# A graph convolution whose end rows are turned and multiplied in strips of 128 columns

## The chip, the cores and the metric

The kernel runs on one core of a Trainium2 chip. The metric is the device time of one execution in microseconds (us). The engines are called TensorE (PE in the rows; PEld is its weight load), VectorE (DVE), ScalarE (ACT), GpSimd (POOL) and SyncE (SP, its DMA queue SPq). TensorE's clock is granted at one of two levels, shown as 0.5 (1.2 GHz) or 1.0 (2.4 GHz).

## What is computed

Four graph layers run one after the other on 12500 nodes with 64 features and 200000 edges, sorted by their target node: an attention layer, a gated layer, a polynomial layer and a block of three convolutions. The change touches the last:

```python
def conv(h, W, b):
    m = jnp.concatenate([h[dst], h[src], edge_attr], axis=1) @ W + b
    return jax.ops.segment_sum(m, dst, num_segments=n_nodes)
h = jax.nn.relu(conv(x, W1, b1))
h = jax.nn.relu(conv(h, W2, b2))
return conv(h, W3, b3)
```

The sum over the edges of a node can be drawn in front of the product. With deg the number of edges into a node, its output row is deg * (h @ W[0:64]) + (sum of h[src]) @ W[64:128] + (sum of the attributes) @ W[128:144] + deg * b. The kernel computes it in this way; the sums of the attributes are the same for all three convolutions.

## The kernel before, in words

Nodes lie in 98 tiles of 128 (`T` = 98), edges in 128 rows of `J` = 1564 columns, in 68 chunks of 23 columns (`NC`, `C`). `conv_layer` is called three times, with k = 0, 1, 2, and has a chunk part and an end part. All loops of it are unrolled; each engine has its own instruction stream, and semaphores order them.

*Chunk part.* GpSimd fetches h[src] for 23 columns, one indirect DMA of 128 rows a column (`gather_columns`, line 864), into one of two buffers. ScalarE (`take`, lines 2089 to 2097) spreads the flags that mark where a node's edges begin, brings in the 16 edge attributes where k is 0 (line 2096) and the gathered rows (2097). VectorE runs a segmented sum along the edges (2235: three scans of up to 32 features in the first convolution, two in the others). ScalarE puts the running sums back in row order (`give`, 2102) and SyncE stores them to a table in DRAM (2059), 80 columns wide in the first convolution and 64 in the others. In the first 33 chunks the node term is computed beside that, three tiles a chunk: ScalarE scales H by deg (`scale`, 2107; where k is over 0 it also copies 17 columns that hold the attribute sums and deg, 2109), TensorE turns the tile (2159), ScalarE copies it (2116), TensorE multiplies by `g.Wz` (2168), ScalarE copies the product into `z` (2121).

*End part.* A carry across the 128 edge rows is turned, scanned and turned back (2173, 2240, 2175), and one fixed row is corrected in the table (2023, 2247, 2025). Then GpSimd fetches for every tile the row at which each node's edges end, 98 indirect DMAs into `cat` (2032). Tiles are worked in units: eleven of 8 tiles, two of 4 and one of 2. For each unit TensorE turns the rows in PSUM (`turn_rows`), ScalarE copies them to SBUF (2147), TensorE multiplies (`multiply_rows`), VectorE adds `z` (2256) and, where k is 0, keeps the attribute sums (2261), ScalarE applies the ReLU (2140) and SyncE stores the unit (2067). TensorE's order is t0, then t(q+1) and m(q) for each unit q; the buffers form a ring of 2 where k is 0 and of 3 otherwise. ScalarE's order is copy(q), then ReLU(q-1).

The shapes differ. Where k is 0, each tile is 81 columns wide (64 sums, 16 attribute sums, deg), is turned by itself (2192) and multiplied by `g.Wt` with 64 output columns (2204). The column for deg is written into `cat` by VectorE once all chunks are stored (2244), and TensorE waits for that (`s_degs`). Where k is over 0, two tiles of 64 columns are turned at once (2188) and multiplied by a block diagonal of the weights in `g.Wkv` with 128 output columns (2200).

The weights of the convolutions are loaded in the first phase, near its end: twelve small DMAs on SyncE's queue (lines 433 to 440, issued by `load`, line 384), between the stores of a node table (422) that ScalarE's copies wait for (540).

## Time and profile before

| | us |
|---|---|
| median of 3 runs | 13276.4 |
| lowest and highest | 13261.65, 13276.62 |
| the profiled execution | 13250.52 |
| its span, first to last instruction | 13248.7 |
| busy: GpSimd | 9102.4 (69%) |
| busy: VectorE | 4039.7 (30%) |
| busy: ScalarE | 3484.7 (26%) |
| busy: TensorE | 1392.0 (11%) |

The page of the profile has the busy time of each engine, the costliest groups of instructions and the DMA queues. A busy share is a mean over phases with different limits. Which wait sets the end of a phase is read from the timeline, which lists instructions in order of time with the idle time before them and what ended it; "issue" there means that the profile shows nothing the engine waited for. Runs of like instructions are merged, with their count. A float32 product is recorded as two MATMUL instructions, and each has a LDWEIGHTS of its own.

### The profile page before, as it was taken

To read this page: it belongs to the slowest core of one execution; us is meant where nothing else is said; L and a number is where in the kernel's file an instruction comes from. 1 tells how busy PE (TensorE), PEld (TensorE's weight loads), DVE (VectorE), ACT (ScalarE), POOL (GpSimd) and SP (SyncE) were. 2 spreads that over 40 slices of the span, in tenths; PEclk is the share of its full clock that TensorE was granted. 3 is DMA by queue.
4 is the path that set the end of the run, shared out by engine and by line. 5 is a ranking of instruction groups with operands and counts; after the bars stand their busy time and mean duration, and the time that the engine had idled before them with its cause. 6 is when DMAs were issued, how large, how long until landed. Compare 5 with 4: busy or idle time off the path is not lost. (4 is left out here: it accounts for less than half of the span.)

```text
span 13248.7 us, 37564 instructions
## 1 busy us (share of the span) xinstructions
PE 1392.0 (11%) x6735; PEld 1006.9 (8%) x6735; DVE 4039.7 (30%) x5465; ACT 3484.7 (26%) x4624; POOL 9102.4 (69%) x8728
## 2 busy tenths in 40 slices
PE   5200000030000000395000000200000000000000
PEld 3100000010000000273000000100000000000000
DVE  2255555544544544695111111011111101111110
ACT  2322322312222222275332222122211212221121
POOL 4677777757777776402777777577777767777776
PEclk8655555555555555697555555555555555555555
DMA  7333333313333333001222222111111111111111
GB/s 283 132 99 95 95 100 96 95 31 89 94 99 95 94 94 87 14 1 31 62 58 61 58 58 58 42 50 46 49 46 46 48 39 50 46 49 46 46 48 42
DMA packets 404824, 919.06 MB, mean 69 GB/s; under 512 B 171046, under 2 KB 195277, under 8 KB 389496
## 3 DMA queue, kind: packets, MB, share of 16 engines
q0 software_dynamic: 278944, 386.91, 13.3%
q1 hardware_dynamic: 121832, 529.42, 10.9%
q14 instruction: 176, 1.44, 0.0%
q10 hardware_dynamic: 3824, 0.50, 0.0%
q8 instruction: 48, 0.79, 0.0%
HBM read 456.45 MB, written 459.77 MB: 69 GB/s over the span
## 5 line engine op out<-in xcount | busy, mean ns | idle before, releaser
L864 POOL DMA_INDIRECT arena<-tab,src x6256 | 6544.2, 1046 | 2893.7 <-issue 2103.0
L2235 DVE TENSOR_TENSOR_SCAN arena<-cv_keep,arena 128x768 f32<-128x768 f32 (+1 forms) x476 | 752.0, 1627 | 5754.5 <-issue 4533.5
L864 POOL DMA_INDIRECT arena<-tab,spread x1564 | 1651.7, 1056 | 510.2 <-issue 510.2
L2097 ACT COPY arena<-arena 128x1472 f32<-128x1472 f32 x204 | 545.3, 2673 | 3002.8 <-DMA arena<-tab,src 3002.8
L2102 ACT COPY arena<-arena 128x1472 f32<-128x1472 f32 (+1 forms) x204 | 588.4, 2884 | 552.4 <-DVE arena L2235 463.2
L1089 PE MATMUL e_t<-ident,arena 128*68 128x128 f32 (+1 forms) x2 | 0.8, 394 | 4426.1 <-PEq L1424 2216.7
L2159 PE MATMUL cv_t<-ident,arena 128*81 128x128 f32 (+1 forms) x294 | 138.0, 469 | 2912.8 <-ACT arena L2109 1671.9
L2096 ACT COPY arena<-arena 128x368 f32<-128x368 f32 x68 | 55.3, 813 | 1351.3 <-issue 1322.7
L2173 PE MATMUL cv_t<-ident,arena 128*64 128x128 f32 (+1 forms) x3 | 1.3, 425 | 3391.4 <-ACT arena L2102 3391.4
L951 ACT ACTIVATE ae_prob<-arena 128x92 f32<-128x92 f32 x68 | 17.1, 251 | 1228.4 <-issue 942.8
L1874 DVE TENSOR_SCALAR arena<-arena 128x448 bf16<-128x448 f16 x1252 | 325.2, 329 | 43.2 <-issue 21.1
L1493 DVE TENSOR_TENSOR arena<-arena,ge_small 128x23 f32<-128x23 f32 x68 | 13.3, 195 | 1065.3 <-DMA arena<-tab,src 1065.3
L1089 PEld LDWEIGHTS e_t<-ident,arena 128*68 128x68 f32 (+1 forms) x2 | 0.3, 131 | 4426.4 <-issue 4426.4
L1757 PE MATMUL po_u<-arena,Hn 128*128 128x448 bf16 x1564 | 301.4, 355 | 289.7 <-DVE Hn L1864 289.7
L1025 DVE TENSOR_TENSOR arena<-arena,ae_prob 128x1472 f32<-128x1472 f32 x68 | 260.1, 3825 | 219.6 <-issue 215.5
L1456 ACT ACTIVATE ge_decay<-arena 128x768 f32<-128x768 f32 x68 | 56.4, 830 | 1015.0 <-issue 902.1
L992 DVE TENSOR_TENSOR_SCAN ae_work<-ae_keep,arena 128x768 f32<-128x768 f32 x136 | 240.1, 1765 | 221.8 <-remote 146.6
L1757 PE MATMUL po_u<-arena 128*128 128x448 bf16 x1564 | 298.8, 352 | 0.2 <-DVE arena L1874 0.2
L943 ACT ACTIVATE ae_work<-arena 128x768 f32<-128x768 f32 x136 | 208.4, 1533 | 300.8 <-issue 261.0
L2159 PEld LDWEIGHTS cv_t<-ident,arena 128*81 128x81 f32 (+1 forms) x294 | 53.9, 183 | 2949.7 <-ACT arena L2109 1683.0
L1034 DVE TENSOR_TENSOR_SCAN arena<-ae_work,arena 128x768 f32<-128x768 f32 x136 | 238.8, 1756 | 115.2 <-issue 101.7
L1497 DVE TENSOR_TENSOR arena<-arena,ge_small 128x1472 f32<-128x1472 f32 x68 | 258.7, 3804 | 0.2 <-issue 0.2
(369 smaller groups left out, 7017.6 us busy)
## 6 DMA issues: line engine op xcount, KB each, us to landing
rows<-arena SPq DMA_DIRECT2D x68, 1506.5 KB
arena<-tab,src POOLq DMA_INDIRECT x6256
rows3b<-arena SPq DMA_DIRECT2D x136, 736.0 KB
rows<-arena SPq DMA_DIRECT2D x68, 920.0 KB
rows<-arena SPq DMA_DIRECT2D x68, 828.0 KB
tab<-arena SPq DMA_DIRECT2D x49, 1024.0 KB
q_start<-arena SPq DMA_DIRECT2D x32, 1564.0 KB
arena<-q_start SPq DMA_DIRECT2D x68, 736.0 KB
```

The costliest lines, as they stand in the source:

```text
L864: pool.indirect_dma_start(out=rows[b][:, j, :], out_offset=None, in_=table, in_offset=bass.IndirectOffsetOnAxis(ap=idx[:, at:at + 1].bitca ...
L943: return nc.scalar.activation(works.rearrange("p (h d) j -> p h d j", h=HH), args[:, 0, :, h0:h0 + HH].rearrange("p j h -> p h j").unsquee ...
L992: v.tensor_tensor_scan(out=work[:, :], data0=keep[:, :], data1=qts[:, x * HF * C1:(x + 1) * HF * C1], initial=0.0, op0=ALU.mult, op1=ALU.a ...
L1025: v.tensor_tensor(mix[:, :, 1:C1].rearrange("p (h d) j -> p j h d", h=H), kv[:, :, D:2 * D].rearrange("p j (h d) -> p j h d", h=H), prob.u ...
L1034: ins = v.tensor_tensor_scan(out=part, data0=work[:, :], data1=part, initial=0.0, op0=ALU.mult, op1=ALU.add)
L1497: v.tensor_tensor(peak[:, :, 1:C1].rearrange("p f j -> p j f"), r[:, :, D:2 * D], pre.unsqueeze(2).to_broadcast([P, C, D]), ALU.mult).then ...
L1757: ins = nc.tensor.matmul(ps_u[:, x, 0:half], wide[c % 2][:, x * P:x * P + P, j], ring[:, n % RING, :], start=(n == 0), stop=(n == J - 1))
L1874: v.tensor_scalar(ring[:, n % RING, :], iota_hi, hi[:, n:n + 1], None, ALU.is_equal).then_inc(s_hot, 1)
L2097: nc.scalar.copy(chain[:, 0:D, 1:C1], rin[b].rearrange("p j f -> p f j")).then_inc(s_in, 1)
L2102: nc.scalar.copy(rows.rearrange("p j f -> p f j"), chain[:, :, 1:C1]).then_inc(s_copied, 1)
L2159: nc.tensor.transpose(ps_t[b][0:K_Z, 0:P], hd[b][:, 0:K_Z], g.ident[:, :]).then_inc(s_tr, 1)
L2235: ins = v.tensor_tensor_scan(out=part, data0=keep[:, 0:(f1 - f0) * C1], data1=part, initial=0.0, op0=ALU.mult, op1=ALU.add)
```

## The change

It does five things.

- In the first convolution the rows of a unit, 8 tiles of 80 columns, are taken as one run of 640 columns and turned in 5 strips of 128, across the borders of the tiles. `windows_of` works out which tiles a strip touches. Strip by strip the turned rows are multiplied by a block that holds the weights of those tiles at their place and zeros elsewhere, and the products are added in PSUM. The first strip's block has the full 512 output columns, so that it also starts the sum; the others have 192, 128, 192 and 128. The units of 4 and of 2 tiles end in a strip of 64 and of 32 rows, for which ScalarE makes a second copy.
- The second and third convolution go the same way through the code. For their width of 64 no strip crosses a pair of tiles: shapes and counts stay as they were.
- The blocks are cleared by VectorE at the start of each convolution and filled by small DMAs on SyncE's queue, 12 in the first convolution and 8 in the others (2 before); TensorE waits for them before the end part. `g.Wkv` is no longer written there.
- The constant column moves: where k is 0, ScalarE copies deg beside the scaled tile (one more instruction a tile), `g.Wz` has the bias in its 65th row, and the product with `g.Wz` is 65 deep. VectorE's copy into `cat` and `s_degs` are gone, and `cat` is 80 columns wide.
- `g.Wt` is gone with four of the twelve loads of the first phase.

```diff
             for k in range(3):
                 wk = a[f"L3_gnn_W{k + 1}"]
                 load(g.Wz[0:D, k, :], wk[0:D, :], s_wconv)
-                load(g.Wt[0:D, k, :], wk[D:2 * D, :], s_wconv)
-                to = g.Wz if k else g.Wt
-                load(to[D:D + ED, k, :], wk[2 * D:2 * D + ED, :], s_wconv)
-                load(to[D + ED:K17, k, :], a[f"L3_gnn_b{k + 1}"].rearrange("(a f) -> a f", a=1), s_wconv)
+                if k:
+                    load(g.Wz[D:D + ED, k, :], wk[2 * D:2 * D + ED, :], s_wconv)
+                bias = K17 - 1 if k else D
+                load(g.Wz[bias:bias + 1, k, :], a[f"L3_gnn_b{k + 1}"].rearrange("(a f) -> a f", a=1), s_wconv)
...
+def windows_of(width):
+
+    parts = []
+    for x in range(UNIT):
+        for m in range(x * width // P, -(-(x + 1) * width // P)):
+            c0, c1 = max(x * width, m * P), min((x + 1) * width, (m + 1) * P)
+            parts.append((m, x, c0 - m * P, c1 - m * P, c0 - x * width))
+    count = UNIT * width // P
+    first = [min(x for m, x, *_ in parts if m == w) for w in range(count)]
+    after = [max(x for m, x, *_ in parts if m == w) + 1 for w in range(count)]
+    shared = any(first[w + 1] < after[w] for w in range(count - 1))
+    if shared:
+        after[0] = UNIT
+    spans = [(x, y - x) for x, y in zip(first, after)]
+    return shared, spans, [(m, x - first[m], r0, r1, w0) for m, x, r0, r1, w0 in parts]
...
-    turned = UNIT * P // (2 if paired else 1)
+    turned = UNIT * width
+    shared, spans, parts = windows_of(width)
+    assert UNIT * D <= 512 and len(spans) * P == turned
...
-    cat, at = view(g, at, T, K_T)
+    cat, at = view(g, at, T, width)
+    blocks = [None] * len(spans)
+    for m, (_, count) in enumerate(spans):
+        blocks[m], at = view(g, at, count * D)
...
-            if paired:
-                wait(sp, s_blank, 1)
-                for half in (slice(0, D), slice(D, P)):
-                    sp.dma_start(g.Wkv[half, k - 1, half], a[f"L3_gnn_W{k + 1}"][D:2 * D, :]).then_inc(s_pair, 16)
             wait(sp, s_init, 1)
             if k == 0:
                 for c in range(2):
                     load_attrs(c)
+            wait(sp, s_blank, 1)
+            rows_in = a[f"L3_gnn_W{k + 1}"][D:D + width, :]
+            for m, slot, r0, r1, w0 in parts:
+                sp.dma_start(blocks[m][r0:r1, slot * D:slot * D + D], rows_in[w0:w0 + r1 - r0, :]).then_inc(s_block, 16)
...
-                ins = nc.scalar.activation(hd[b][:, 0:D], g.H[:, t, :], ACT.Copy, scale=g.deg[:, t:t + 1])
-                if k:
-                    ins = nc.scalar.copy(hd[b][:, D:K17], g.E17[:, t, :])
-                ins.then_inc(s_scaled, 1)
+                nc.scalar.activation(hd[b][:, 0:D], g.H[:, t, :], ACT.Copy, scale=g.deg[:, t:t + 1])
+                extra = g.E17[:, t, :] if k else g.deg[:, t:t + 1]
+                nc.scalar.copy(hd[b][:, D:K_Z], extra).then_inc(s_scaled, 1)
...
-            depth = P if paired else K_T
             for q, tiles in enumerate(units):
-                n = len(tiles) * P // (2 if paired else 1)
                 act.wait_ge(s_ctr, q + 1)
                 wait(act, s_cmm, q - ring + 1)
-                nc.scalar.copy(ht[q % ring][0:depth, 0:n], ps_t[q % ring][0:depth, 0:n]).then_inc(s_cht, 1)
+                whole, over = divmod(len(tiles) * width, P)
+                n = whole * P
+                if over:
+                    nc.scalar.copy(ht[q % ring][0:over, n:n + P], ps_t[q % ring][0:over, n:n + P])
+                nc.scalar.copy(ht[q % ring][:, 0:n], ps_t[q % ring][:, 0:n]).then_inc(s_cht, 1)
...
-            if k == 0:
-                pe.wait_ge(s_degs, 1)
 
             def turn_rows(q):
                 tiles = units[q]
                 pe.wait_ge(s_end[q], 16 * len(tiles))
                 wait(pe, s_cht, q - ring + 1)
-                if paired:
-                    for x, t in enumerate(tiles[::2]):
-                        ins = nc.tensor.transpose(ps_t[q % ring][:, x * P:x * P + P], cat[:, t:t + 2, :].rearrange("p a f -> p (a f)"),
-                                                  g.ident[:, :])
-                else:
-                    for x, t in enumerate(tiles):
-                        ins = nc.tensor.transpose(ps_t[q % ring][0:K_T, x * P:x * P + P], cat[:, t, :], g.ident[:, :])
+                flat = cat[:, tiles.start:tiles.stop, :].rearrange("p t f -> p (t f)")
+                for first in range(0, len(tiles) * width, P):
+                    deep = min(len(tiles) * width - first, P)
+                    ins = nc.tensor.transpose(ps_t[q % ring][0:deep, first:first + P], flat[:, first:first + deep], g.ident[:, :])
                 ins.then_inc(s_ctr, 1)
 
             def multiply_rows(q):
                 pe.wait_ge(s_cht, q + 1)
                 wait(pe, s_sum, q - ring + 1)
-                if paired:
-                    for x in range(len(units[q]) // 2):
-                        ins = nc.tensor.matmul(ps_o[q % ring][:, x * P:x * P + P], ht[q % ring][:, x * P:x * P + P],
-                                               g.Wkv[:, k - 1, :], start=True, stop=True)
-                else:
-                    for x in range(len(units[q])):
-                        ins = nc.tensor.matmul(ps_o[q % ring][:, x * D:x * D + D], ht[q % ring][0:K_T, x * P:x * P + P],
-                                               g.Wt[0:K_T, k, :], start=True, stop=True)
+                n = len(units[q])
+                used = [m for m in range(len(spans)) if m * P < n * width]
+                for m in used:
+                    first, count = spans[m]
+                    count = min(count, n - first)
+                    deep = min(n * width - m * P, P)
+                    ins = nc.tensor.matmul(ps_o[q % ring][:, first * D:(first + count) * D],
+                                           ht[q % ring][0:deep, m * P:m * P + P], blocks[m][0:deep, 0:count * D],
+                                           start=not shared or m == 0, stop=not shared or m == used[-1])
                 ins.then_inc(s_cmm, 1)
 
-            if paired:
-                pe.wait_ge(s_pair, 16 * 2)
+            pe.wait_ge(s_block, 16 * len(parts))
...
-            if paired:
-                v.memset(g.Wkv[:, k - 1, :], 0.0).then_inc(s_blank, 1)
...
+            for block_of in blocks:
+                ins = v.memset(block_of, 0.0)
+            ins.then_inc(s_blank, 1)
...
-            if k == 0:
-                dve.wait_ge(s_st, 16 * NC)
-                v.tensor_copy(cat[:, :, K17 - 1], g.deg[:, :]).then_inc(s_degs, 1)
```

## Rows read from the trace of the kernel before

**Rows 1.** The page, costliest groups: line, engine, operation, tiles, count | busy, mean | idle

```profile
L864 POOL DMA_INDIRECT arena<-tab,src x6256 | 6544.2, 1046 | 2893.7 <-issue 2103.0
```

**Rows 2.** Line 864 alone: stretch and length, busy (count), granted clock, DMA share, GB/s

```profile
6171.90:6315.60 143.70, 108.59 (x115) 0.50 0.23 60
...
7431.50:7592.50 161.00, 123.16 (x115) 0.50 0.22 59
```

**Rows 3.** Line 2032: duration minimum/median/maximum, first and last start

```profile
L2032 POOL DMA_INDIRECT arena<-rows,end_i x98: 940/945/967, 8355.2 to 8476.4; - x98
```

**Rows 4.** Timeline, first convolution's end part: start, us, engine, line [idle before <-releaser]

```profile
8387.69 1.01 ACT L2147 COPY arena<-cv_t 81x1024 f32<-81x1024 f32 x1 [18.13 <-issue]
...
8432.56 0.69 DVE L2256 TENSOR_TENSOR Hn<-arena,cv_o 128x512 f32<-128x512 f32 x1 [80.08 <-issue]
...
8454.89 1.01 ACT L2147 COPY arena<-cv_t 81x1024 f32<-81x1024 f32 x1 [20.98 <-issue]
...
8461.88 0.26 PE L2204 MATMUL cv_o<-Wt,arena 81*128 81x64 f32 x1 [2.52 <-issue]
...
8497.59 0.69 DVE L2256 TENSOR_TENSOR Hn<-arena,cv_o 128x512 f32<-128x512 f32 x1 [64.20 <-DMA dst_tab<-arena]
...
8502.02 0.69 DVE L2256 TENSOR_TENSOR Hn<-arena,cv_o 128x512 f32<-128x512 f32 x1 [3.61 <-DMA dst_tab<-arena]
```

**Rows 5.** Timeline, the same end part, catch-up and last instruction

```profile
8526.80 0.69 DVE L2256 TENSOR_TENSOR Hn<-arena,cv_o 128x512 f32<-128x512 f32 x1 [4.21 <-PE cv_o L2204]
...
8546.77 0.31 ACT L2140 ACTIVATE Hn<-Hn 128x128 f32<-128x128 f32 x1 [0.30 <-DVE Hn L2256]
```

**Rows 6.** PE, PEld, DVE, ACT, POOL: busy (count) in stretches, granted clock, DMA share, GB/s

```profile
8503.00:8546.00 43.00, 43.00 (x206) 43.00 (x206) 7.53 (x20) 14.02 (x20) 0.00 (x0) 0.50 0.16 59
...
13232.00:13238.00 6.00, 6.00 (x29) 6.00 (x30) 1.95 (x3) 1.94 (x4) 0.00 (x0) 0.50 0.43 131
...
13238.00:13244.80 6.80, 4.14 (x36) 3.92 (x35) 2.99 (x6) 1.01 (x3) 0.00 (x0) 1.00 0.63 190
```

**Rows 7.** Timeline, second convolution's end part

```profile
10810.14 0.69 DVE L2256 TENSOR_TENSOR Hn<-arena,cv_o 128x512 f32<-128x512 f32 x1 [32.84 <-remote]
...
10843.74 0.69 DVE L2256 TENSOR_TENSOR Hn<-arena,cv_o 128x512 f32<-128x512 f32 x1 [32.91 <-issue]
...
10854.07 0.94 POOL L2032 DMA_INDIRECT arena<-rows3b,end_i  x1 [0.30 <-issue]
...
10881.67 1.28 DVE L2256 TENSOR_TENSOR Hn<-arena,cv_o 128x512 f32<-128x512 f32 x2 [5.04 <-remote]
```

**Rows 8.** Timeline, first phase, where TensorE multiplies 512 columns at a time

```profile
302.80 1.99 PE L623 MATMUL fp_tab<-Wrel,arena 64*128 64x512 f32 x8 [2.46 <-ACT arena L540]
...
304.72 0.66 PE L595 MATMUL fp_turn<-ident,arena 128*128 128x128 f32 x4
...
318.01 0.37 ACT L529 COPY arena<-fp_kv 128x256 f32<-128x256 f32 x1 [10.64 <-remote]
...
329.27 2.05 ACT L540 COPY arena<-fp_tab 128x512 f32<-128x512 f32 x4 [10.72 <-remote]
...
331.47 3.78 PE L623 MATMUL fp_tab<-Wrel,arena 64*128 64x512 f32 x8 [15.31 <-issue]
```

**Rows 9.** Timeline, first phase, SyncE's queue and ScalarE around the weight loads

```profile
401.24 1.86 SPq L384 DMA_DIRECT2D Wt<-in_L_gnn_W_dram  x2
...
403.98 0.60 SPq L384 DMA_DIRECT2D Wt<-in_L_gnn_W_dram  x1
...
408.44 1.09 SPq L422 DMA_DIRECT2D tab<-arena  x2
...
412.39 1.07 ACT L540 COPY arena<-fp_tab 128x512 f32<-128x512 f32 x2 [4.19 <-DMA tab<-arena]
```

**Rows 10.** Timeline of ScalarE in a chunk of the first convolution; line 2109's durations

```profile
6209.75 3.31 ACT L2102 COPY arena<-arena 128x1840 f32<-128x1840 f32 x1 [1.84 <-issue]
...
L2109 ACT COPY arena<-E x196: 188/194/200, 8551.6 to 11941.6; 128x17 f32<-128x17 f32 x196
```

More of the change, by code:

```diff
@@ L154, in alloc @@
     g.Wz = sb("Wz", [P, 3, D])
-    g.Wt = sb("Wt", [P, 3, D])
     g.E17 = sb("E17", [P, T, ED + 1])
@@ L446, in _ @@
             wait(sp, s_look, 16)
-            wait(sp, s_wconv, 16 * 12)
+            wait(sp, s_wconv, 16 * 8)
             wait(sp, s_qdone, 16 * (FULL + 1))
@@ L1969, in conv_layer @@
     s_scaled, s_tr, s_ht, s_mm, s_z = map(sem, ("scaled", "turned", "turned_copied", "multiplied", "z"))
-    s_last, s_chain, s_back, s_put, s_degs, s_zx = map(sem, ("last_turned", "chain", "carry_back", "put", "degs", "zx"))
+    s_last, s_chain, s_back, s_put, s_zx = map(sem, ("last_turned", "chain", "carry_back", "put", "zx"))
     s_ctr, s_cht, s_cmm, s_sum, s_relu, s_out = map(sem, (
@@ L1975, in conv_layer @@
     s_row = pool_sem(g, "fixed_rows")
-    s_blank, s_pair = sem("pair_blank"), sem("pair_in")
-    paired = k > 0
+    s_blank, s_block = sem("blocks_blank"), sem("blocks_in")
     units = units_of([UNIT] * 11 + [4, 4, 2])
-    ring = 3 if paired else 2
+    ring = 3 if k else 2
     s_end = [pool_sem(g, f"ends{n}") for n in range(len(units))]
@@ L1982, in conv_layer @@
     table_rows = g.rows3 if k == 0 else g.rows3b
-    K_Z = D if k == 0 else K17
-    K_T = K17 if k == 0 else D
+    K_Z = D + 1 if k == 0 else K17
     at = 0
@@ L2031, in _ @@
                     ends = bass.IndirectOffsetOnAxis(ap=g.end_i[:, t:t + 1].bitcast(U32), axis=0)
-                    pool.indirect_dma_start(out=cat[:, t, 0:width], out_offset=None, in_=table_rows, in_offset=ends)\
+                    pool.indirect_dma_start(out=cat[:, t, :], out_offset=None, in_=table_rows, in_offset=ends)\
                         .then_inc(s_end[n], 16)
```

## The prediction

> **What bounds the kernel now.** I began with the costliest groups of the page. GpSimd's column gathers (line 864) lead everything: 6256 of them, 1046 ns each, and GpSimd has nothing else to wait for in their loops [rows 1]. The stretches of that line show their pace: 115 gathers (five chunks) take 143.7 us early in the first convolution and 161.0 us later, so 1.25 us and then exactly 1.40 us each [rows 2]. The change takes nothing from these loops. It works in the end part of the convolution, where 98 gathers fetch the end rows. Their own line says that they start between 8355.2 and 8476.4 us, so again 1.25 us apart [rows 3].
>
> The timeline of that end part shows that the gathers do not set its end. Name the units by number: t for turning, m for multiplying. A full unit before has 8 transposes and 8 float32 multiplications, each of the latter recorded twice, and a weight load beside each record: 2 x (8 + 16) = 48 records. The copy of t1 starts at 8387.69, the sum of m0 at 8432.56, the copy of t2 at 8454.89, the sum of m1 at 8497.59 [rows 4]. Between these lie 32, 16 and 32 TensorE records: 1.40, 1.40 and 1.33 us for each. TensorE's own rows carry single multiplications here, each 0.26 us long after 2.54 us of idle, and a weight load lies half-way: again one record per 1.40 us [rows 4]. I call this the crawl. It does not come from the shape: with 128 columns the second convolution has 24 records a unit, and its sums are 33.6 us apart, 24 x 1.40 [rows 7]. Then it is over: the sum of m2 comes at 8502.02, 4.4 us after that of m1 though 48 records lie between [rows 4]. In the second convolution the fast sums begin at 10881.67, after a last gather at 10854.07 [rows 7]: 27.6 us, against 25.6 us here (8502.02 - 8476.4 [rows 3, 4]). So the end of the crawl hangs on the gathers, not on how much TensorE has done. That fits a resource which handles one item of GpSimd and one of TensorE per 1.40 us, and which the 1.25 us gathers leave with a backlog. I cannot see the resource; I use only its pace and its end.
>
> After 8502 TensorE alone counts: sums of full units from 8502.02 to 8526.80 are five units, 4.96 us each, and the last ReLU starts at 8546.77 and takes 0.31 us [rows 4, 5]. In 8503 to 8546 TensorE is busy throughout at a granted clock of 0.50 (1.2 GHz), 206 records in 43 us, 0.21 us each [rows 6].
>
> **The change, part by part.**
>
> *End rows in strips.* A unit of 8 rows of 80 is 640 columns, turned as 5 strips instead of 8 tiles. The products have 512, 192, 128, 192 and 128 columns. Each is recorded twice again, so a unit has 2 x (5 + 10) = 30 records. During the crawl the same number is handled: by 8497.59 that were 112 before (t0, t1, m0, t2, m1: 16 + 16 + 32 + 16 + 32). After the change, 112 records cover t0, t1, m0, t2, m1, t3, m2, t4 (10 + 10 + 20 + 10 + 20 + 10 + 20 + 10 = 110). So at the crawl's end m2 is complete, TensorE has run m3 ahead, and can do m4, since t4 is turned. Before, m2 was the last one it had done. Left at 8502 are m5 to m10 and the three small units, against m3 to m10 and the small ones: 6 full units instead of 8.
>
> Next the pace of a full unit at 1.2 GHz. Records of up to 128 columns: 0.21 us [rows 6]. A 512-column record: eight took 3.78 us with the clock low, last one's tail included, hence 0.39 to 0.47, I take 0.43; at full clock eight start within 1.92 us, 0.24 each, and four transposes take 0.66 us with the tail, 0.12 each [rows 8]. 192 columns show nowhere: between 0.21 and 0.43, linear 0.25. Sum: 9 x 0.21 + 2 x 0.43 + 4 x 0.25 = 3.75 us against 4.96. At 2.4 GHz: 9 x 0.12 + 2 x 0.24 + 4 x 0.14 = 2.1 us. ScalarE's copy shrinks from 1024 columns (1.01 us [rows 4]) to 640, some 0.65 us; with the ReLU it needs 1.3 us a unit and stays covered by TensorE.
>
> Which clock? Before, it stayed at 0.50 for all 43 us of the catch-up. The third convolution, whose units have 128-column products, has 0.50 in 13232 to 13238 and 1.00 in 13238 to 13244.8, 36 records in 4.14 us busy [rows 6]. The new units stream more columns for each record than those. I therefore take 6 us at 1.2 GHz, then 2.4 GHz. The Trainium skill (TensorE: Matmul & The Clock Gate, Part 4) says that transposes do not bring the full clock the way matmuls do; by that rule too, 5 transposes beside wider products warm more readily than 8 beside 64-column ones, and the trace agrees as far as the rows above go.
>
> Sum: m5 can start about 8504.2 (release 8502, ReLU, copy and two signals). 6 us at 3.75 are 1.6 units; the other 4.4 at 2.1 are 9.2 us. The three small units took 5.4 us before (45.06 us from 8502.02 to the end less 8 x 4.96); with 24 records for 30 and the higher clock 4.5. Last sum and ReLU 0.6. End 8524.5 instead of 8547.1: -22.6 us. With the clock low throughout: 22.5 + 5.3 + 0.6, end 8532.6: -14.5 us.
>
> The Trainium skill (FP8 and Floating Point Precision, TensorE Precision Notes) puts true FP32 at four passes through the array. That speaks against this change, which multiplies 1152 columns a unit instead of 512: an estimate by it is 1152 x 4 / 1.2 GHz = 3.84 us for the products alone, 4.9 us with the transposes, and the gain would shrink to some 6 us. The trace disagrees: two records per product, and 0.86 us for a 512-column pair.
>
> *Weight loads of the first phase.* Four of twelve go from SyncE's queue: 1.24 + 0.58 us (the pair of 1.86 with its gap), 0.60, 0.60: 3.1 us, 3.2 with gaps. Behind them stands the table store at 408.44, and ScalarE sits idle 4.19 us for its buffer, until 412.39 [rows 9]. All of it can be won or, if a later store sets that phase, none: 0 to -3.2. The row is direct, so -3.
>
> *Edits that I cost at nothing.* The constant's 98 small copies on ScalarE: 0.19 us each by the nearest row, 18.6 us in all. Three a chunk are 0.57 us, and ScalarE idles 1.84 us before it gives the chunk back, waiting for the scans [rows 10]; without that cover +18.6. The 12 block loads on SyncE in the first convolution, 12 x 0.60 [rows 9] = 7.2 us, and 8 for 2 in the others: queued behind their wait is the chunk loop's first store, due after a chunk of 28.7 us [rows 2]. VectorE's clearing of the blocks stands ahead of its first scan, which is due as late. TensorE's wait for the blocks comes 2 ms later. The constant's copy on VectorE (one instruction) lay beside the flight of the fixed row. Transposes of 65 for 64 columns: less than one record's spread. Second and third convolution keep shapes and record counts.
>
> Total -22.6 - 3 = -25.6 us. The profiled execution took 13250.5 us (span 13248.7 and 1.8 around it), so 13224.9 by its own scale. The median of the three runs is 25.9 us above it; I carry the difference over: 13276.4 - 25.6 = 13250.8, say 13251. A measurement of this kernel tells about 0.2%, 26.6 us, from no change: the forecast lies just inside.
>
> **The rivals.**
>
> *Clock stays low* (0.22): for it, 43 us of full work at 0.50 before [rows 6]; against, the third convolution. -14.5 and 0 to -3: 13259 to 13262.
>
> *Column cost twice what I take* (0.03): -6 to -9, 13268. Against: rows 8.
>
> *The crawl disappears* (0.07), because 30 records a unit no longer feed it. Then gathers bind: the last starts at 8476.4, some 5 us of chain behind it, end 8482: -65 - 3, 13208. Against: 24 records a unit still crawl [rows 7].
>
> *The change does not do what it says* (0.06): the crawl also counts columns, so that fewer, wider records pass no faster. Against it stand 16 records of 512 columns between two copies of ScalarE at 318.01 and 329.27, 0.70 us each, no dearer than others [rows 8]. Then only the catch-up's pace gains, 8 x 1.2 = 10 us: 13266.
>
> *Slower* (0.07): ScalarE itself is held to one instruction per 1.40 us in the chunk loop, as TensorE is. It has 14 a chunk while tiles are multiplied, 17 after the change. The point is 23 a chunk (32.2 / 1.40 [rows 2]); beyond it each costs 1.40 us, three in 33 chunks +139 us, net 13389. It decides only if waits count as items too. Against: TensorE's waits do not count in the crawl's arithmetic, and ScalarE idles between chunks.
>
> *Rest* 0.03, spread over noise.
>
> **How the numbers follow.** Forecast 0.52. It straddles the border, since its terms are good to some 6 us: half beyond -0.2%. Faster: 0.26 of it, 0.07 (crawl gone), 0.03 from the low-clock case and the rest: 0.36. Slower 0.07. Same: the rest, 0.57. The range leaves out the crawl's disappearance and the slower case, 0.14 together, and a little noise: 13226 (the forecast with the clock up from the start, and a run as low as the profiled one) to 13277 (no gain, the median of before).
>
> **What would show it.** The profile after should have 1.40 us per TensorE record until about 8495, sums of m0, m1 and m2 before it, the burst near 8499, full units 3.7 us apart and then 2.1 with the clock at 1.00, end of the first convolution 22 us after the burst. A table store at 405 instead of 408.4 shows the first phase. I am wrong if the crawl's end moves with TensorE's work, if the 512-column records cost more than 0.47 us at low clock, or if chunks become longer than 32.2 us.

## The result and the profile after

The changed kernel took 13249.8 us (median of 19 runs, 13238.1 to 13256.6), the kernel before 13276.4 us beside it (19 runs, 13261.7 to 13279.5): ratio 0.9981, 95% interval 0.9975 to 0.9987, so -26.6 us. That is 1 us from the forecast. The interval leaves out no change; the forecast had put the border of what can be told at 0.2%, 26.6 us. The profiled execution took 13253.4 us (span 13251.6).

The chain that the rows before told of comes back with its lines shifted: gathers of end rows are line 2051 (before 2032 [rows 3]), sums 2269 (2256 [rows 4]), turning 2207, multiplying 2219, ScalarE's copy 2167. The line of the end gathers (minimum/median/maximum duration in ns, first and last start):

```profile
L2051 POOL DMA_INDIRECT arena<-rows,end_i x98: 943/947/970, 8381.5 to 8502.9; - x98
```

And the timeline of the end part (start, us, engine, line, operation, [idle before <-releaser]). First the crawl:

```profile
8403.87 3.69 PE L2219 MATMUL cv_o<-arena 128*128 128x512 f32 x10
...
8412.80 1.33 PE L2207 MATMUL cv_t<-ident,arena 128*128 128x128 f32 x5 [5.24 <-DMA arena<-rows,end_i]
...
8425.00 0.69 DVE L2269 TENSOR_TENSOR Hn<-arena,cv_o 128x512 f32<-128x512 f32 x1 [46.26 <-remote]
...
8438.99 0.69 ACT L2167 COPY arena<-cv_t 128x640 f32<-128x640 f32 x1 [12.64 <-issue]
...
8466.99 0.69 DVE L2269 TENSOR_TENSOR Hn<-arena,cv_o 128x512 f32<-128x512 f32 x1 [41.16 <-remote]
...
8481.02 0.69 ACT L2167 COPY arena<-cv_t 128x640 f32<-128x640 f32 x1 [12.68 <-remote]
...
8509.01 0.69 DVE L2269 TENSOR_TENSOR Hn<-arena,cv_o 128x512 f32<-128x512 f32 x1 [41.20 <-remote]
```

then the burst and the catch-up:

```profile
8527.98 0.69 DVE L2269 TENSOR_TENSOR Hn<-arena,cv_o 128x512 f32<-128x512 f32 x1 [18.14 <-PE cv_o L2219]
...
8528.72 0.68 DVE L2269 TENSOR_TENSOR Hn<-arena,cv_o 128x512 f32<-128x512 f32 x1
...
8529.97 3.87 PE L2219 MATMUL cv_o<-arena 128*128 128x512 f32 x10 [2.81 <-ACT arena L2167]
...
8533.87 0.69 DVE L2269 TENSOR_TENSOR Hn<-arena,cv_o 128x512 f32<-128x512 f32 x1 [4.33 <-PE cv_o L2219]
...
8536.38 0.69 DVE L2269 TENSOR_TENSOR Hn<-arena,cv_o 128x512 f32<-128x512 f32 x1 [1.68 <-PE cv_o L2219]
...
8543.91 0.69 DVE L2269 TENSOR_TENSOR Hn<-arena,cv_o 128x512 f32<-128x512 f32 x1 [1.68 <-PE cv_o L2219]
...
8550.54 0.31 ACT L2158 ACTIVATE Hn<-Hn 128x128 f32<-128x128 f32 x1 [0.23 <-DVE Hn L2269]
```

Read three things. Sums of m0, m1 and m2 (8425.00, 8466.99, 8509.01) are 42.0 us apart, 30 records of 1.40. The finer steps fit too: 8425.00 to 8438.99 (t2, 10 records) is 14.0, to 8466.99 (m1, 20 records) 28.0, to 8481.02 14.0, to 8509.01 28.0. And the burst comes 25.1 us behind the last gather (8527.98 - 8502.86), as 25.6 before. From it to the end of the last ReLU are 22.9 us; before they were 45.1 [rows 4, 5].

The stretches (us, length, busy (count) of PE, PEld, DVE, ACT, POOL, granted clock, DMA share, GB/s) tell of the clock:

```profile
8528.00:8533.00 5.00, 3.03 (x7) 2.00 (x8) 1.54 (x4) 2.32 (x4) 0.00 (x0) 0.69 0.29 106
8533.00:8541.00 8.00, 8.00 (x49) 6.55 (x49) 2.48 (x6) 3.64 (x6) 0.00 (x0) 0.98 0.18 67
8541.00:8549.00 8.00, 7.96 (x47) 6.09 (x46) 3.00 (x8) 4.03 (x11) 0.00 (x0) 1.00 0.34 127
```

It is at 1.00 where the kernel before stayed at 0.50 for 43 us [rows 6]. From the first end gather to the first column gather of the second convolution the time is 173.7 us (8381.5 to 8555.2) against 196.8 (8355.2 to 8552.0): -23.1 us, forecast -22.6. The end parts of the other two convolutions are 0.9 and 1.0 us shorter (167.9 against 168.8 us, and 153.1 against 154.1 to the last sum), with the same counts of records; I had left them at nothing, and no run shows the reason. The profiled first phase was 20 us longer after the change (its first gather of line 863 started at 509.8), but another execution of the old first phase, in the experiment e8 below, shows the same:

```profile
L863 POOL DMA_INDIRECT arena<-tab,spread x1564: 941/952/1795, 509.8 to 2671.2; - x196
```

```profile
L864 POOL DMA_INDIRECT arena<-tab,spread x1564: 940/949/1799, 508.3 to 2670.2; - x196
```

So two single profiles can't be subtracted whole here, and the first phase least of all.

### The profile page after: what moved, and what is told of

Same layout as the page of the kernel before. It is cut to its first block and busy times, and to the rows that moved or that the text cites. A ratio compares the mean times of both kernels' runs of the same rounds, so it can differ in the third digit from the quotient of the medians.

```text
span 13251.6 us, 37484 instructions
## 1 busy us (share of the span) xinstructions
PE 1346.6 (10%) x6630; PEld 978.0 (7%) x6630; DVE 4042.0 (31%) x5475; ACT 3487.8 (26%) x4725; POOL 9100.0 (69%) x8728
## 3 DMA queue, kind: packets, MB, share of 16 engines
q14 instruction: 177, 1.45, 0.0%
```

## The experiments

Executions differ by chip in a way that no profile of one chip could show. On some chips the kernel before takes about 13270 us, on others about 11895 us. The first kind is called crawling here. Each result names its kind; the first two profiles are of that kind.

**Four kernels on a chip that does not crawl** (before: 11893.3 us). All start from the changed kernel.

e1, 48 records a unit:

```
                 ins = nc.tensor.transpose(ps_t[q % ring][0:deep, first:first + P], ...)
+            if k == 0 and len(tiles) == UNIT:
+                for extra in range(9):
+                    x = extra % 5 * P
+                    ins = nc.tensor.transpose(ps_t[q % ring][:, x:x + P], flat[:, x:x + P], g.ident[:, :])
             ins.then_inc(s_ctr, 1)
```

> The changed kernel, but each full unit of the first convolution's end part turns nine of its strips a second time into the same place: 48 TensorE records a unit as before the change, in place of 30; loads, column and products stay changed. My theory (the crawl handles one record per 1.40 us whatever its shape): the sums of the first units come 67 us apart instead of 42.0, about m2 is done when the crawl ends, as before the change, and 8 full units of some 4.7 us follow: first convolution some 20 us longer than after the change, time about 13270. Rival (the crawl counts work or columns, and the change gained by something else): sums stay about 42 us apart and only the catch-up lengthens, 6 units by 2.2 us, 13 us in all: about 13263.

Measured: 11892.2 us, ratio 0.9999 (0.9990 to 1.0008). Sums some 10 us apart, the pace of 8 gathers, so neither the theory nor its rival was put to the test.

e2, TensorE starts when all end rows are there:

```
             pe.wait_ge(s_block, 16 * len(parts))
+            for q, tiles in enumerate(units):
+                pe.wait_ge(s_end[q], 16 * len(tiles))
```

> The changed kernel, but in all three convolutions TensorE waits for all 98 end gathers before it turns the first unit. My theory (a backlog of the gathers, which ends some 25 us after the last of them, holds TensorE to one record per 1.40 us): in the first convolution some 16 records crawl for 23 us after the last gather, then 14 units follow at 2.5 us and less, so the last ReLU comes about 59 us after the last gather instead of 48; with the same in the other two, total 13270 to 13285. Rival (TensorE is held only by what it queued while gathers were being issued): no crawl at all, the last ReLU some 38 us after the last gather, and the total about 30 us below the changed kernel's: 13220.

Measured: 11957.3 us, ratio 1.0053 (1.0040 to 1.0067): +64 us, since no TensorE work of the end parts hides beside the gathers. Last sum 36.3 us behind the last gather in the first convolution. Full units 2.51 us each, with TensorE never idle and the clock up:

```profile
7673.00:7693.00 20.00, 20.00 (x122) 16.15 (x121) 6.61 (x16) 9.69 (x16) 0.00 (x0) 1.00 0.28 106
```

e3, the first convolution's end gathers replaced by SyncE's plain loads of consecutive rows, so that it adds up wrong rows:

```
+                sp.dma_start(cat[:, t, :], table_rows[t * P:t * P + P, :]).then_inc(s_plain[n], 16)
```

> The changed kernel, but the first convolution's 98 end gathers by GpSimd are left out: SyncE loads 98 tiles of consecutive rows of the same table by plain transfers into the same places, so the first convolution adds up the wrong rows. My theory (GpSimd's indirect gathers make the crawl): no record per 1.40 us, units follow SyncE's loads, 8 x 0.6 = 4.8 us a unit, and the end part of the first convolution lasts some 66 us instead of 173.7: about -105 us. Rival (TensorE crawls there by itself, for instance for want of its instructions): the sums of m0, m1, m2 stay 42 us apart.

Measured in a single run: 11819.0 us, 74 us less than the kernel before. Sums 2.4 to 6.5 us apart. It says nothing on the crawl, for want of one.

e4, spaced gathers:

```
                     pool.indirect_dma_start(out=cat[:, t, :], ...).then_inc(s_end[n], 16)
+                    if k == 0:
+                        pool.memset(idle, 0.0).then_inc(s_idle, 1)
+                        pool.wait_ge(s_idle, t + 1)
```

> The changed kernel, but after each of the first convolution's 98 end gathers GpSimd clears a scratch tile of 512 columns and waits for that, so that the gathers start some 2 us apart instead of 1.25. My theory (a resource needs 1.40 us for each gather, and gathers 1.25 us apart pile up): at 2 us nothing piles up, TensorE gets records at 1.40 us or faster, keeps up with the gathers, and the last ReLU comes within 10 us of the last gather: end part some 196 + 10 us instead of 173.7, about +32 us. Rival (the crawl is a fixed tail of some 25 us behind the last gather, whatever their pace): last ReLU 45 us or more after the last gather, +65 us.

Measured in a single run: 11943.8 us, 50.5 us more; gathers 1.78 us apart, last sum 6.7 us behind the last gather. That is about the same as without spacing (7.1 in e1).

None of the four could decide what it was made for; together they showed that the crawl belongs to the chip.

**The change, and one part of it, on chips that do not crawl.** The column alone, made from the kernel before (the bias also goes to `g.Wz`, `s_degs` and VectorE's copy are gone, the twelve loads stay):

```
-    K_Z = D if k == 0 else K17
-    K_T = K17 if k == 0 else D
+    K_Z = D + 1 if k == 0 else K17
+    K_T = R3 if k == 0 else D
...
+                extra = g.E17[:, t, :] if k else g.deg[:, t:t + 1]
+                nc.scalar.copy(hd[b][:, D:K_Z], extra).then_inc(s_scaled, 1)
```

> The changed kernel as it is, to stand beside the kernel before on the chip of this call. The chip of the first experiments ran the kernel before in 11893 us: gathers stayed 1.25 us apart in all loops and in its end parts TensorE kept up with them, without the crawl. My theory (the gain was made of records that pass at 1.40 us in the crawl, and of the catch-up behind it): on such a chip the end part is bound by the gathers, last ReLU 5 to 7 us after the last of them before and after the change, and the change gives 0 to -5 us (ratio 0.9996 to 1.0000); where the end part crawls as in the first profile, -25 us again. Rival (the gain is due to the narrower work itself, whatever the chip): -20 us or more on either.

> The kernel before with the constant column moved alone: in the first convolution the end tiles are turned and multiplied 80 wide, one by one as before, and ScalarE copies the constant beside the scaled rows, 98 times in the chunk loop; the twelve loads stay. My theory: the 98 copies of 0.19 us lie in ScalarE's idle time, 0 us against the kernel before (within 5). Rival (uncovered): +18.6 us. The rival by which ScalarE is held to one instruction per 1.40 us would give +139 us.

Measured beside 11900.6 us: changed 11899.6 (ratio 0.9998, 0.9989 to 1.0008), column alone 11900.9 (1.0000, 0.9991 to 1.0009). On a third such chip both again:

> The changed kernel as it is, again, to stand beside the constant column alone on one chip. Where the end parts crawl (kernel before near 13260 to 13276 us): first convolution's end part 23 us shorter than before, first phase 2 to 3 us, ratio 0.9980. If instead the two first profiles differed for another reason than the strips, within 10 us of the kernel before. Where nothing crawls (before near 11893 us): -1 us again.

> The kernel before with the constant column moved alone (tiles still turned and multiplied one by one, 48 records a unit, twelve loads), again. Where the end parts crawl, my theory: its sums keep the 65 us between m0 and m1 and the end part its 196.8 us, the 98 copies on ScalarE cost nothing there too, since the resource sets the chunk at 32.2 us: within 5 us of the kernel before, so that the strips carry the whole gain. Rival (moving the column is part of the gain, since a signal of VectorE and a wait of TensorE before the first turn are gone): 5 to 20 us faster than before. Rival (the copies join what the resource must serve, 1.40 us each): +137 us. Where nothing crawls: 0 us again.

Measured beside 11892.7 us: 11891.2 and 11892.4 (both 0.9999, 0.9990 to 1.0008). The change is worth -1 to -1.5 us there by the medians, which is within the noise. Why, in the stretch of the first convolution's end part, first the column alone, whose tiles are still multiplied one by one as before the change:

```profile
7548.00:7676.00 128.00, 63.99 (x294) 59.57 (x294) 10.52 (x28) 20.49 (x28) 92.62 (x98) 0.50 0.24 55
```

then the changed kernel:

```profile
7548.00:7676.00 128.00, 58.58 (x187) 43.21 (x187) 10.54 (x26) 16.37 (x30) 92.58 (x98) 0.65 0.23 55
```

TensorE is busy in half of the stretch in either; 98 gathers at 1.25 us set it. A third fewer instructions off the critical path buy nothing. That the new copies of the constant cost nothing is shown for these chips: 98 of them, unchanged time.

The chip of e12 did not crawl either, so its rival, that moving the column is part of the gain on chips that do, stays without a run. The first two profiles speak against it. Before the change VectorE's copy, for which TensorE waited, was over at 8349.8:

```profile
8349.51 0.25 DVE L2244 COPY arena<-deg 128x98 f32<-128x98 f32 x1 [2.77 <-DMA rows<-arena]
```

The first turning started at 8366.55, 11.3 us behind the first end gather; after the change it starts 11.4 us behind it (8392.88).

**On a crawling chip: the kernel before with TensorE held back (e8), and the loads (e6)** (before: 13276.8 us). e8 has the edit of e2 in the kernel before. e6 adds to the changed kernel:

```
+            for n in range(16):
+                load(g.idle[n % 2 * D:n % 2 * D + D, n // 2, :], a["L3_gnn_W1"][D:2 * D, 0:16], s_wconv)
```

> The kernel before with the wait of the second experiment: in all three convolutions TensorE starts its first unit when all 98 end gathers have landed, so that each end part shows TensorE's own pace, with no gather beside it. In the changed kernel this gave 2.51 us a full unit in the first convolution at a granted clock of 1.00, and its last sum 36.3 us behind the last gather. My theory (the strips do less work for TensorE, and bring the full clock, which 8 tiles and 64-column products do not): 5.04 us a full unit at a clock of 0.50, last sum 11 x 5.04 + 5.4 + 7 = 68 us behind the last gather, total about 32 us above that kernel's. Rival (before would have come to the full clock as well, had it not crawled): some 2.9 us a unit, last sum 42 us behind, total 6 us above. Rival (the wider products cost what the strips save): 2.5 us a unit, the same total.

> The changed kernel with sixteen more loads (64 x 16 elements, into scratch) behind the eight that were left in the first phase, four times what the change took away. My theory (each load delays the table stores behind it, and by them the whole phase): 16 x 0.6 = 9.6 us more between the last table store ahead of the loads and the next one (7.2 us in the changed kernel), and the same 8 to 10 us on the total. Rival (the table stores do not set the end of that phase): the store is late, the total is the changed kernel's within 2 us.

e8 measured 13287.1 us, ratio 1.0008 (0.9999 to 1.0018). Its timeline, behind the last gather, is the most telling of all:

```profile
8503.12 0.94 POOL L2032 DMA_INDIRECT arena<-rows,end_i  x1 [0.30 <-issue]
...
8505.90 3.43 PE L2192 MATMUL cv_t<-ident,arena 128*81 128x128 f32 x16 [132.04 <-DMA arena<-rows,end_i]
...
8507.91 1.01 ACT L2147 COPY arena<-cv_t 81x1024 f32<-81x1024 f32 x1 [135.44 <-PE cv_t L2192]
...
8509.17 1.90 PE L2204 MATMUL cv_o<-Wt,arena 81*128 81x64 f32 x16
...
8510.90 1.05 PE L2192 MATMUL cv_t<-ident,arena 128*81 128x128 f32 x8
8524.19 1.01 ACT L2147 COPY arena<-cv_t 81x1024 f32<-81x1024 f32 x1 [15.27 <-remote]
...
8528.57 0.69 DVE L2258 TENSOR_TENSOR Hn<-arena,cv_o 128x512 f32<-128x512 f32 x1 [149.32 <-DMA dst_tab<-arena]
```

TensorE had been idle for 132 us, and it does not crawl: t0, t1, m0 and t2 are done by 8512. But ScalarE gets to copy t1, whose turning ended at 8509.3, only at 8524.19, and VectorE sums m0, done at 8511.1, at 8528.57, 25.4 us behind the last gather. So what crawls are the signals behind TensorE's records, and the backlog was there though TensorE had added nothing in this end part: the gathers made it. After that, full units are 5.04 us apart, clock 0.50:

```profile
8530.00:8570.00 40.00, 40.00 (x192) 40.00 (x192) 6.36 (x16) 13.82 (x17) 0.00 (x0) 0.50 0.16 60
```

That was my expectation, except that the tail is 76.5 us where I wrote 68 for a chip without crawl. (The total of e2, to which the expectation compares, is from the other kind of chip, so only the units are compared here.)

e6 measured 13261.3 us, ratio 0.9988 (0.9978 to 0.9997), against 0.9981 of the change on the first chip. SyncE's queue:

```profile
418.09 0.34 SPq L422 DMA_DIRECT2D tab<-arena  x1
...
424.51 10.05 SPq L384 DMA_DIRECT2D idle<-in_L_gnn_W_dram  x16
434.61 0.58 SPq L444 DMA_DIRECT2D end_tab<-end_i  x1
435.61 1.09 SPq L422 DMA_DIRECT2D tab<-arena  x2
```

From store to store 17.5 us. In the changed kernel the same two stores are 7.2 us apart (418.55 and 425.73), in the kernel before 9.5 (398.98 and 408.44); the profiles of e9 and e8 have the same 7.2 and 9.5. Sixteen loads give +10.3 us there, and relative to the kernel before beside each +11 us on the median (-15.5 against -26.6), though the intervals overlap. So a load delays the store by 0.65 us, and four by 2.3 us (the two profiles) to 2.6 (this dose). How much of it reaches the total is less sure: the first column gather starts at 516.0 us with the sixteen loads and at 509.8 in the changed kernel, 6 us for 10, and at 508.3 in e8, which has all twelve loads.

**On another crawling chip: three end parts, three edits (e9)** (before: 13275.8 us). The edits are those of e1 in the first, e4 in the second, e3 in the third convolution, and, in the first, 16 copies of one column each at the end of ScalarE's chunk. The third convolution adds up wrong rows, as in e3.

> The changed kernel with one edit in each convolution's end part, read part by part. First: nine strips of each full unit turned a second time (48 TensorE records a unit, not 30), and 16 small copies more on ScalarE in each of its 68 chunks. Second: GpSimd clears a scratch tile after each end gather and waits for it, gathers 1.78 us apart. Third: the end gathers are left out, SyncE loads 98 tiles of consecutive rows by plain transfers (the last sums add wrong rows). Where the end parts crawl (kernel before near 13276 us), my theory (one record per 1.40 us, whatever its shape; gathers 1.25 us apart leave a backlog that ends 25 us behind the last): first, sums 67.2 us apart instead of 42.0, from first end gather to the next convolution's gathers 188 us instead of 173.7; second, no backlog, sums 14.2 us apart instead of 33.6, last sum 5 to 8 us behind the last gather instead of 40.8; third, end part to the last sum 66 us instead of 153. Rivals: first, the crawl counts work, sums stay 42 apart; second, it is there whenever gathers are in flight, sums 33.6 apart or more; third, TensorE crawls by itself, sums 33.6 apart. The 16 copies: nothing, chunks stay 32.2 us; if ScalarE were held to one instruction per 1.40 us, chunks of 46 us. Where nothing crawls (before near 11893 us), by either theory the second part is 52 us longer and the third some 60 us shorter.

Measured: 13201.3 us, ratio 0.9942 (0.9926 to 0.9959). Part by part; first the sums with 48 records a unit:

```profile
8486.42 0.69 DVE L2290 TENSOR_TENSOR Hn<-arena,cv_o 128x512 f32<-128x512 f32 x1 [96.91 <-remote]
...
8536.77 0.69 DVE L2290 TENSOR_TENSOR Hn<-arena,cv_o 128x512 f32<-128x512 f32 x1 [49.53 <-remote]
...
8542.87 0.69 DVE L2290 TENSOR_TENSOR Hn<-arena,cv_o 128x512 f32<-128x512 f32 x1 [4.54 <-PE cv_o L2240]
...
8546.36 0.69 DVE L2290 TENSOR_TENSOR Hn<-arena,cv_o 128x512 f32<-128x512 f32 x1 [2.67 <-PE cv_o L2240]
```

m0 comes 94.1 us behind the first gather (8392.3); in the changed kernel it was 43.5. The difference, 50.6 us, is the 36 records that t0 and t1 have more, at 1.40 us. The interval of 67.2 us that I expected could not appear, because the burst (8536.77, 23.4 us behind the last gather) came before m1 was through. The end part took 182.8 us (forecast 188) against 173.7. The 18 records a unit, in the crawl and in the catch-up together, are thus worth 9.1 of the 23.1 us: they leave eight full units for the catch-up instead of six, and a unit takes 3.49 us there instead of 2.51.

The other 14.0 us lie between this run and the kernel before, at equal counts of records. 11.0 of them are the way from the burst to the last sum, 33.4 us against 44.4: a full unit takes 3.49 us at a clock of 1.00 (8546.4 to 8563.8) here and 5.04 at 0.50 before. 2.2 are an earlier burst (23.4 against 25.6 us behind the last gather), for which no run shows a reason. The clock rose though a unit has 14 turnings here, more than the 8 of before:

```profile
8537.00:8571.00 34.00, 33.05 (x198) 27.28 (x196) 9.36 (x26) 13.79 (x27) 0.00 (x0) 0.92 0.22 82
```

Second, spaced gathers:

```profile
L2056 POOL DMA_INDIRECT arena<-rows3b,end_i x98: 949/949/964, 10756.1 to 10932.7; - x98
```

```profile
10807.31 0.69 DVE L2290 TENSOR_TENSOR Hn<-arena,cv_o 128x512 f32<-128x512 f32 x1 [53.98 <-PE cv_o L2240]
10821.40 0.69 DVE L2290 TENSOR_TENSOR Hn<-arena,cv_o 128x512 f32<-128x512 f32 x1 [13.40 <-PE cv_o L2240]
```

14.1 us apart instead of 33.6, the last 5.8 us behind the last gather instead of 40.8. At 1.82 us a gather there is no crawl. Third, plain loads: sums 2.4 to 4.0 us apart, and the part from the last column gather to the last sum 79.2 us (13106.1 to 13185.3) instead of 179.6. No gathers, no crawl; I had written 66 us from its start, counted from the loads (it was 52.9 from the first load at 13132.4).

Fourth, ScalarE: from the ninth chunk until the tiles are multiplied, chunks were 29.8, 42.7, 28.7 and 28.7 us in turn, 32.5 on average; after that seven of 28.7, then 32.2. Something does stall now and then (GpSimd is idle for up to 14 us), but the gathers run at 1.25 us afterwards and mostly make it up: the loop took 2172.1 us against 2161.7 in the changed kernel, +10 us for 1088 copies, where one per 1.40 us would have given 46 us a chunk. Forecast: nothing.

**A version with paced gathers (e10)**, on a third crawling chip (before: 13259.9 us): the edit of e4 with a tile of 160 columns, in all three convolutions.

> The changed kernel, but in the end parts of all three convolutions GpSimd clears a scratch tile of 160 columns after each gather and waits for it: gathers about 1.45 us apart instead of 1.25. It slows the gathers to make the end come earlier. My theory (the resource takes 1.40 us for a gather and leaves a backlog only when they come faster, and the records of TensorE pass almost free when there is none): on a chip that crawls (kernel before near 13276 us) the last gather starts 141 us after the first, sums keep 11.6 us apart, the last one 6 to 7 us behind the last gather; first convolution 20 us, second 14 us, third 6 us shorter than in the changed kernel: about 13210, ratio 0.995. Rival (TensorE's records take their share of the resource, so that 1.45 us still leaves a backlog): sums 30 us apart or more, the burst some 25 us behind the last gather, 13250 to 13290. On a chip that does not crawl (before near 11893 us) either theory gives only the slower gathers, 3 x 20 us: about 11955.

Measured: 13219.0 us, ratio 0.9971 (0.9959 to 0.9983): 41 us less than before, where the change alone gave 27 on the first chip. End parts of 161.8, 164.7 and 151.3 us against 173.7, 167.9 and 153.1: -17 us, not the -40 expected. The crawl is gone (sums 10.2 to 12.7 us apart, the last 6.8 us behind the last gather), but GpSimd itself stalls ten gathers in, and gathers are 1.54 us apart on average (1.47 between the stalls), not 1.45:

```profile
8377.35 0.95 POOL L2053 DMA_INDIRECT arena<-rows,end_i  x1 [0.27 <-issue]
...
8380.46 0.95 POOL L2053 DMA_INDIRECT arena<-rows,end_i  x1 [1.92 <-remote]
...
8383.96 0.95 POOL L2053 DMA_INDIRECT arena<-rows,end_i  x1 [2.31 <-remote]
...
8386.06 0.95 POOL L2053 DMA_INDIRECT arena<-rows,end_i  x1 [0.91 <-POOL arena L2055]
```

It is faster than the kernel before where the end parts crawl. That it beats the changed kernel there is told by these parts alone: the two did not run side by side, and their ratios (0.9971 and 0.9981) have intervals that overlap. Where nothing crawls, its 3 x 97 gathers come 0.22 us later each, some +64 us (worked out, not run; by the same reckoning e4, with 97 gathers 0.53 us later, comes to +51, and it measured +50.5). So it is no version for every chip.

## Why the prediction came out right

*The crawl: size right, reading wrong.* "TensorE handles one record per 1.40 us" held to a tenth of a us in every interval from m0's sum on, and so did its indifference to shape. But I took it for TensorE's pace. The rows above show m0 multiplied at 8403.87 to 8407.6 at ordinary speed and its sum 17.4 us later (for m1 it is 49 us, 8417.7 to 8466.99): it is the way from TensorE's records to the waiting engine that passes one per 1.40 us, and TensorE is held up only when it has run far enough ahead, as in [rows 4]. That its end hangs on the gathers, with a backlog behind it, is shown by e8. That it needs gathers close together is shown by e9 and e10: it is there at 1.25 us and gone at 1.47 and 1.82.

*What is left at the burst: right.* m3 and m4 came in the burst, six full units and three small ones were left.

*Pace of a full unit: wrong at both clocks.* I had 3.75 us cold (at the low clock) and 2.1 at full clock. Measured at full clock: 2.51. The cold one in the groups of one unit (m2's multiplications), and the same products at full clock:

```profile
L2219 PE MATMUL cv_o<-arena 128*128 128x512 f32 x2 | 2.1, 1142 | 15.6 <-ACT arena L2167 15.6
L2219 PE MATMUL cv_o<-arena 128*128 128x192 f32 x4 | 1.7, 527 | 0.0
L2219 PE MATMUL cv_o<-arena 128*128 128x128 f32 x4 | 1.3, 421 | 0.0
```

```profile
L2219 PE MATMUL cv_o<-arena 128*128 128x512 f32 x2 | 1.0, 594 | 0.0
L2219 PE MATMUL cv_o<-arena 128*128 128x192 f32 x4 | 1.0, 325 | 0.0
L2219 PE MATMUL cv_o<-arena 128*128 128x128 f32 x4 | 0.8, 273 | 0.0
```

The means are durations, and these overlap; a price is read from the starts. Products take 4.01 us from first start to next turn when cold (8439.73 to 8443.74) and turning 1.1 more: 5.1 us, no less than the 5.04 of before. From start to start a 512-column record takes 0.85 us cold (8440.75 to 8441.60) and 0.43 at full clock (8534.22 to 8534.65), about twice what I took. The failed step is the reading of [rows 8]. Its eight records in 1.99 us are pairs that run at once, each on 64 of the 128 rows ("64*128" in the row); a window of 0.2 us of the kernel before holds two of them, 0.70 us in all:

```profile
302.80 0.70 PE L623 MATMUL fp_tab<-Wrel,arena 64*128 64x512 f32 x2 [2.46 <-ACT arena L540]
```

Stretch by count gave me half of the price of a product that has the array for itself, as those of the strips do. The Trainium skill (TensorEngine Tiling (Array Packing), Key Properties) says that different tiles of the array can work in parallel; the trace agrees. And the rule that I set aside was right: four passes for FP32 (the Trainium skill, FP8 and Floating Point Precision, TensorE Precision Notes) gives, as an estimate, 3.84 us cold and 1.92 at 2.4 GHz for the 1152 columns; measured 4.01 and 1.96 (8534.22 to 8536.18). The rival "column cost twice" had a chance of 0.03 and its mechanism was true. Its time was not: -6 to -9 us is what six units at 4.9 us give (8504.2 + 29.4 + 5.3 + 0.6 = 8539.5, so -7.6), with the clock low throughout, which the rival does not say. With the measured prices and the clock as forecast the sum is -19.7.

*The clock: right in kind, earlier than I wrote, and it hid the wrong prices.* I gave it 6 us of work from the start of m5; it rose before the ten products of m5 were through (3.70 us from their first start to the next turning, 8529.97 to 8533.67, against 4.01 cold; the granted clock is 0.69 in 8528 to 8533, 0.98 behind it). Lead 2.0, m5 3.9, five units 12.3, small ones 4.0, last ReLU 0.6: 22.9 us before rounding, against my 22.5. The six full units took 16.2 us of it. I had 15.2; with the measured prices and my 6 us of low clock it would have been 18.1 (6 us, then 4.8 units of 2.51). So prices too low by 2.9 us met a clock that came early, which was worth 1.9 us, and the lead and the small units gave back 0.7 more. That this part came out within 1 us is luck in good part. Since cold units gain nothing, the rival "clock stays low" would have been worth only the two full units fewer, some 10 us (2 x 5.04), not 14.5. e8 shows that the old form stays down by itself: 40 us of unbroken work with 81-row tiles and 64-column products stay at 0.50. Neither the count of records nor that of turnings is the reason (e9); which other trait of the form is, no run tells.

*First phase: right at the queue.* The store comes 2.3 to 2.6 us earlier, by the profiles and by the dose, for 3; that all of it reaches the total is not shown.

*What cost nothing: right.* The column alone is at 1.0000 where nothing crawls; the blocks' loads and memsets show in no chunk: chunks keep 32.2 us. On the crawling chip the first convolution's loop, from its first column gather to its last, took 2161.7 us with the 98 copies against 2160.3, and the loops of the other two, which got none, are longer by as much (2161.4 and 2161.2 against 2160.1 and 2160.0). So the rival of +139 us is refuted there, as it is by the 16 copies a chunk of e9.

*The sum.* -23.1, -0.9 and -1.0 in the end parts and up to -2.3 in the first phase are -25.0 to -27.3 us by the profiles, -26.6 by the medians. The share that I did not see at all is the chip: the same edits are worth 1 us where gathers don't crawl. A median "before" from one chip said nothing of that.

## What to carry to other kernels

When an engine seems slow, compare the end of its instruction with the start of what waits for it: an instruction that ends on time and is noticed 17 us later asks for fewer records or fewer requests upstream, not for less arithmetic. But price what follows once the queue is empty too: here 14 of the 23.1 us came at equal counts of records, most of them from the clock that the new form brings. A price per instruction worked out as stretch by count is only good if the instructions don't overlap, so look for a row of the same tile shape, and at the clock of its stretch. A trace of one chip is a sample: a gain that rests on a queue found there has to be measured on another.

## What the runs showed of the hardware

Chips differ by 11% on one program. Of the 1352 us between the spans of two profiles of the changed kernel (13251.6 and 11899.2 us), 1043 lie in the five loops of column gathers, and 118 in the first phase, ahead of the first column gather. Line 863 in 161 us of the first convolution (POOL busy (count), granted clock, DMA share, GB/s), changed kernel, first on the crawling chip, then on the other:

```profile
7000.00:7161.00 161.00, 122.91 (x116) 0.50 0.22 59
```

```profile
7000.00:7161.00 161.00, 121.70 (x130) 0.50 0.24 63
```

A gather's median duration differs little (952 ns in the row of the first phase above, 945 on the other chip); but on the one they follow each other at 1.40 us, on the other at 1.25. On the crawling chip, too, the first seven chunks of a loop go at 1.25 us (28.7 us a chunk [rows 2]), as if something filled up before it held GpSimd back. Three chips of each kind came up, beside the chip of the first two profiles, which may be one of them. On the crawling ones end gathers 1.25 us apart leave something behind that delays TensorE's signals until 22 to 28 us past the last gather; with gathers 1.47 us apart and more that was gone.

What this resource is stays open. One candidate can't be excluded by any run here, since each timed run here was recorded with its spans and clock: the writing of records itself. The Trainium skill (NOTIFIC — the notification-queue block, 7.1 Overflow: three behaviours, one of which stalls the engine) says that the block's internal pipeline holds its producers back rather than lose a record; no run here shows it.
